# A decoder layer on one core: feed-forward weights quantised in pieces inside the cross-attention steps, the key rows of ones filled by GpSimd, and the query spread put first in SP's step

## The reference, cut to what matters

```python
x = x + attn(layernorm(x), gamma, Wq, Wkv, Wo)      # 16 heads, causal, rotary
x = x + xattn(layernorm(x), ctx, w_in, ..., 64)     # sequences of 512 places, 8 heads of 16,
                                                    # a band of 64 places on either side
x = x + ffn(layernorm(x), gate_w, down_w, ...)      # inner width 1408
def weight_quant(w):                                # ternary weights
    scale = 1.0 / clip(mean(abs(w)), 1e-5)
    return clip(round(w * scale), -1, 1) / scale
def bit_linear(x, w, g):
    return activation_quant(rms_norm(x, g)) @ weight_quant(w).T
# ffn: gate, up = split(bit_linear(x, gate_w, g1)); h = silu(gate) * up; bit_linear(h, down_w, g2)
```

## Time and profile before

| | |
|---|---|
| median of 3 runs | 1294.87 us (1294.2 to 1295.73) |
| the profiled execution, whole | 1297.97 us |
| its span | 1296.2 us |
| busy in the span | PE 83%, DVE 70%, ACT 43%, GpSimd 40% |
| self-attention ends | about 664 us |
| `setup_cross` | 664 to 684 us |
| `cross` | 684 to 1067 us |
| `setup_ffn` | 1067 to 1093 us |
| `ffn` | 1093 us to the end |

### The profile page before, as it was taken

How to read it: one execution, slowest core, us unless ns; L and a number is a source line. 1 busy time by engine, 2 the same in 40 slices (tenths; PEclk the granted TensorE clock), 3 DMA queues, 4 the chain that set the end, 5 groups by cost and what they waited for, 6 DMA issues and landing times. The chain is left out here.

```text
span 1296.2 us, 24877 instructions
## 1 busy us (share of the span) xinstructions
PE 1072.7 (83%) x9350; PEld 728.7 (56%) x9350; DVE 902.3 (70%) x1709; ACT 554.1 (43%) x887; POOL 515.8 (40%) x461
## 2 busy tenths in 40 slices
PE   0699999999999999999834899999999841777775
PEld 0677677677767667777511566666666520333332
DVE  5577777767777777778743656666666537788884
ACT  3133333333333333333311356656566645555554
POOL 3243434434343444434311134344343333566663
PEclk9989999999999999999975899999999965899998
DMA  8200000000000000000037456646566103000000
GB/s 306 108 1 1 1 1 1 1 1 0 0 0 0 1 0 0 0 0 1 1 135 200 99 117 125 144 120 139 132 130 147 27 24 112 9 24 24 24 25 25
DMA packets 35646, 71.52 MB, mean 55 GB/s; under 512 B 8544, under 2 KB 21344, under 8 KB 31456
## 3 DMA queue, kind: packets, MB, share of 16 engines
q1 hardware_dynamic: 32528, 61.82, 19.0%
q10 hardware_dynamic: 2208, 4.59, 1.0%
q0 software_dynamic: 816, 3.87, 0.8%
HBM read 53.09 MB, written 16.78 MB: 54 GB/s over the span
## 5 line engine op out<-in xcount | busy, mean ns | idle before, releaser
L382 PE MATMUL Yb<-Wo,a_oN 128*128 128x512 f32 x512 | 231.5, 595 | 0.0
L1019 DVE TENSOR_REDUCE mx<-Sm 128x4 f32<-128x768 f32 x128 | 122.4, 956 | 120.0 <-PE Sm L765 119.3
L468 POOL TENSOR_TENSOR a_ql<-a_rot,a_qh 128x512 fp32r<-128x512 f32 x64 | 83.6, 1312 | 183.3 <-ACT a_qh L437 183.3
L861 ACT ACTIVATE x_ex<-Se 128x768 f32<-128x768 f32 x128 | 102.8, 803 | 125.6 <-PE Se L765 125.5
L382 PEld LDWEIGHTS Yb<-Wo,a_oN 128*128 128x128 f32 x512 | 97.1, 191 | 98.5 <-issue 93.4
L315 PE MATMUL Qb<-a_xTh,WqH 128*128 128x256 f32 x512 | 147.0, 287 | 2.4 <-DVE a_vl L569 2.4
L316 PE MATMUL Qb<-a_xTl,WqH 128*128 128x256 f32 x512 | 145.9, 285 | 0.0
L317 PE MATMUL Qb<-a_xTh,WqL 128*128 128x256 f32 x512 | 145.9, 285 | 0.0
L429 ACT ACTIVATE Lb<-Lb 128x512 f32<-128x512 f32 x64 | 37.2, 582 | 253.9 <-PE Ob L374 253.9
L475 POOL TENSOR_TENSOR a_pl<-a_pr,a_ph 128x512 fp32r<-128x512 f32 x64 | 83.7, 1307 | 115.0 <-ACT a_ph L424 115.0
L315 PEld LDWEIGHTS Qb<-a_xTh,WqH 128*128 128x128 f32 x512 | 99.2, 194 | 6.4 <-DVE a_vl L569 3.8
(11 more groups left out here) (196 smaller groups left out, 2524.6 us busy)
## 6 DMA issues: line engine op xcount, KB each, us to landing
K<-k_parts SPq DMA_DIRECT2D x32, 256.0 KB, 7.9
q_parts<-x_qp SPq DMA_DIRECT2D x16, 384.0 KB, 2.6
k_parts<-x_kp SPq DMA_DIRECT2D x16, 384.0 KB, 2.6
Q<-q_parts SPq DMA_DIRECT2D x16, 384.0 KB, 5.0
gate_f<-in_gateT SPq DMA_DIRECT2D x1, 5632.0 KB, 16.1
X<-in_x SPq DMA_DIRECT2D x4, 1024.0 KB, 16.2
Wo<-in_Wo ACTq DMA_DIRECT2D x1, 4096.0 KB, 13.9
Q<-q_parts SPq DMA_DIRECT2D x16, 256.0 KB, 5.7
```

The costliest lines, as they stand in the source:

```text
L382: mm = pe.matmul(Yb[s % 2][:, :], oN[:, s % 2, i * P:(i + 1) * P], t["Wo"][:, HG * u + i, :], start=(i == 0), stop=(i == HG - 1))
L468: pool.tensor_tensor(rot_dst(False, True, par, r), rbuf(par, r)[:, 0:rot_width(r)], rot_dst(True, False, par, r).bitcast(F32), ALU.subtrac ...
L861: act.activation(ex[:, (PAIRS * b + p) % RING, 4 * hf * WIN:4 * (hf + 1) * WIN].rearrange("p (j c) -> p j c", j=2), Se[:, :, 0:2 * WIN], A ...
L1019: dve.tensor_reduce(mx[:, half, at:at + 4].rearrange("p (j a) -> p j a", j=2), Sm[:, :, 0:2 * WIN].rearrange("p j (a c) -> p j a c", a=2), ...
```

## The change

- The weights are cut in 12 pieces: the gate weights in 8 of 1408 columns a partition (704 KB each), the down weights in three of 1536 (768 KB) and one of 1024 (512 KB). Two staging buffers `w_stage` take turns. Every piece is read twice.
- In steps b = 0 to 5, ACT sums the absolute values of two pieces a step, behind the exponentials of slots 1 and 2. In steps 6 to 11, DVE scales and rounds two pieces (slots 0 and 1), ACT writes them as bf16 (slots 1 and 2), and DVE limits them (slots 2 and 7).
- In steps 4 and 6 the sum of a matrix is totalled over the partitions by a matmul in PE's slot 6, and DVE makes the factors from it in its slot 6.
- SP's step is in another order, and the loads of the pieces for the next step stand at its end.
- GpSimd writes the ones of `K` in step -1, after the keys' `low` of sequence 1, and PE waits for them before the first `Se`.
- `setup_ffn` keeps the layer norm's scales alone; SP issues the two norm weights there, not GpSimd.

```diff
+PIECES = [(0, i * F, (i + 1) * F) for i in range(2 * KD)] + [(1, a * D, min(a + 3, KF) * D) for a in range(0, KF, 3)]
+GATES = 2 * KD
+SUM_STEP, QUANT_STEP = 0, 6
...
-            sp.dma_start(t["gate_f32"][:, :].rearrange("p (k n) -> p k n", k=KD),
-                         dram["gateT"].rearrange("(k p) n -> p k n", p=P)).then_inc(t["gate_in"], 16)
...
-            for k in t["K"]:
-                dve.memset(k[ROWS:SHIFTED, :, :], 1.0)
...
+        def summed_at(b):
+            return [n for n in (2 * (b - SUM_STEP), 2 * (b - SUM_STEP) + 1) if 0 <= n < len(PIECES)]
+        def quantised_at(b):
+            return [n for n in (2 * (b - QUANT_STEP), 2 * (b - QUANT_STEP) + 1) if 0 <= n < len(PIECES)]
+        TOTALS = {SUM_STEP + GATES // 2: 0, SUM_STEP + len(PIECES) // 2: 1}
...
+                if (b, s) == (0, 0):
+                    wait(pe, k_ones, len(K))
...
+                    if s == 6 and b in TOTALS:
+                        i = TOTALS[b]
+                        wait(pe, v_ready, b + 2)
+                        wait(pe, w_sized, i + 1)
+                        pe.matmul(Ab[:, 0:1], t["ones"][:, :], w_size[:, i:i + 1], start=True, stop=True).then_inc(w_total, 1)
+                    if s == 7 and b in TOTALS:
+                        wait(pe, w_chain, 2 * TOTALS[b] + 1)
...
-                    if b == B - 1:
...
-                        act.activation(t["junk"][:, :], t["gate_f32"][:, s * n:(s + 1) * n], ACT.Abs,
-                                       accum_out=t["gate_part"][:, s:s + 1]).then_inc(t["gate_sized"], 1)
+                    for n in summed_at(b):
+                        if s == 1 + n % 2:
+                            i, lo, hi = PIECES[n]
+                            wait(act, w_in[n % 2], 16 * (n // 2 + 1))
+                            wait(act, w_summed, n)
+                            act.activation(w_stage[n % 2][:, 0:hi - lo], w_stage[n % 2][:, 0:hi - lo], ACT.Abs,
+                                           accum_out=w_part[:, n:n + 1]).then_inc(w_summed, 1)
+                    for n in quantised_at(b):
+                        if s == 1 + n % 2:
+                            i, lo, hi = PIECES[n]
+                            wait(act, w_rounded, n + 1)
+                            act.activation((t["gateQ"], t["downQ"])[i][:, lo:hi], w_stage[n % 2][:, 0:hi - lo], ACT.Copy,
+                                           bias=-MAGIC).then_inc(w_whole, 1)
...
+                if b == -1:
+                    wait(pool, k_low, b + 3)
+                    for i in range(len(K)):
+                        wait(pool, k_ones, i)
+                        pool.memset(K[i][ROWS:SHIFTED, :, :], 1.0).then_inc(k_ones, 1)
...
             def step(b):
-                if real(b + 2):
-                    keep("k", kp, b + 2, k_low, k_in, K_IN, k_kept)
-                if real(b):
-                    maxima_rows(b, 1)
                 if real(b - 2):
                     wait(sp, y_ready, b - 2)
                     sp.dma_start(ctxb[:, :], dram["ctx"][b - 2]).then_inc(ctx_in, 16)
                 if real(b + 2):
                     spread("q", Q, Q_RUNS, b + 2, q_kept, q_in)
+                    keep("k", kp, b + 2, k_low, k_in, K_IN, k_kept)
+                if real(b):
+                    maxima_rows(b, 1)
+                if real(b + 2):
                     spread("k", K, K_RUNS, b + 2, k_kept, k_in)
                 if real(b + 1):
                     maxima_rows(b + 1, 0)
                 if real(b + 3):
                     keep("q", qp, b + 3, q_low, q_in, Q_IN, q_kept)
+                for n in summed_at(b + 1):
+                    wait(sp, w_summed, n - 1)
+                    load(n)
+                for n in quantised_at(b + 1):
+                    wait(sp, w_summed, len(PIECES))
+                    wait(sp, w_whole, n - 1)
+                    load(n)
...
+            def factors(i):
...
+                wait(dve, w_total, i + 1)
+                dve.tensor_scalar(w_mean[:, i:i + 1], Ab[:, 0:1], 1.0 / (P * width), EPS, ALU.mult, ALU.max).then_inc(w_chain, 1)
...
+            def offset(n):
...
+                wait(dve, w_in[n % 2], 16 * ((len(PIECES) + n) // 2 + 1))
+                dve.tensor_scalar(piece, piece, w_inv[:, i:i + 1], MAGIC, ALU.mult, ALU.add).then_inc(w_rounded, 1)
+            def clip(n):
...
+                wait(dve, w_whole, n + 1)
+                dve.tensor_scalar(piece, piece, 1.0, -1.0, ALU.min, ALU.max)
...
+                    for n in quantised_at(b):
+                        if s == n % 2:
+                            offset(n)
+                        if s == 2 + 5 * (n % 2):
+                            clip(n)
```

More of the change, by code:

```diff
@@ L712, in cross @@
         oN = sb("oN", [P, D], F32)
+        w_stage = [sb(f"w_stage{i}", [P, WIDEST], F32) for i in range(2)]
+        w_part = sb("w_part", [P, len(PIECES)], F32)
+        w_size, w_mean, w_inv = sb("w_size", [P, 2], F32), sb("w_mean", [P, 2], F32), sb("w_inv", [P, 2], F32)
         gate = sb("gate", [P, D], F32)
@@ L1074, in step @@
                         rest(kp, kr, 1, b + 3, k_high, k_low, k_rest)
+                    if s == 3 and b in TOTALS:
+                        size(TOTALS[b])
+                    if s == 6 and b in TOTALS:
+                        factors(TOTALS[b])
+                    for n in quantised_at(b):
[3 more added lines that the diff above has]
+                            clip(n)
                     if b >= B - 1 and s % 2 == 1:
```

133 lines of the change are left out of this document (38 added, 95 removed).

## The result

| | before | after |
|---|---|---|
| median of the runs | 1295.30 us (4 runs) | **1307.85 us** (4 runs, 1303.47 to 1309.85) |
| the profiled execution, whole | 1297.97 us | 1303.47 us |
| its span | 1296.2 us | 1301.7 us |
| steps 0 to 11 | 243.8 us | 287.4 us |

A forecast was written before the change was run, and what follows sets the result against it. Cross steps were taken as PE-bound (92% busy, hiding waits, such as for the keys' spread), the setups by DVE fills and weight quantising. Terms -12.2 + 2.7 + 21 + 1.6 - 1.1 - 6 - 17.3 = -11.3 gave about 1283 us, range 1250 to 1306.

The forecast's parts named there:

- The setup before cross: Before the cross steps: without DVE's three fills the bias sum follows PE directly, -12.2 us.
- the fills on GpSimd: Three fills, 4.6 us each, stand in GpSimd's 21.5 us idle gap ahead of its first maxima work: 0.
- the pipeline's fill: Step -2: the queries' spread goes first, so the keys' keep is issued 2.6 us later; +2.7 us, bounds 0 and +6.
- the setup before the feed-forward steps: After cross: only aggregates, small instructions and two powers at 2.89 us remain; -17.3 us, or -14 with powers as long as before.
- step 15: Last cross step: eight ACT sums, 12.4 us, go, roughly half of them hidden; -6 us, between -4 and -11.
- replace each other, don't add: Steps 6 to 11: DVE's slot 0 load wait delays PE about 2 us, so it finds slot 4's rows nearly there.
- a time of some 1344 us: Rival "the small load is slow", chance 0.03: at the skill's price DVE and ACT wait for every piece, rows land T+19.
- a step lasts 19.05 + 2.0 + 1.0 = 22.05: Steps 0 to 11: no-DMA-wait base, slot 4 stall for maxima rows, clock loss; against 20.3, +21 us, bounds -15 and +44.
- its term for the factors: Steps 4 and 6: DVE stands in slot 6 for PE's total, then three small instructions; +1.6 us, bounds 0 and +4.
- compute alone: Steps 0 to 11: added ACT sums and DVE quantising cost nearly 0, up to +1 us a step if slots don't hold them.
- the sign turns: Steps 0 to 11: from 23.0 us a step on the change is slower, since the other terms give -32.3 us.
- The second rival: Steps 0 to 11, chance 0.25: the 2.9 us stall drops the clock every step; 24.2 us a step, +46, 1309 us.

The follow-up runs named there:

- the run with shifted work: The changed kernel with all sums, roundings, offsets and clips of the weights moved to later slots, mostly by two; median 1319.5 us.
- The run with the order alone: The kernel before with SP's step in the change's order (context rows and queries' spread ahead of keys' keep and maxima rows), no loads; 1295.5 us, ratio 0.9998.
- The run with the cut spread: The changed kernel with loads moved behind key spread and first-half maxima rows, and two of the queries' spread's three transfers put behind the second-half rows; 1253.2 us, the fastest.
- late loads: The changed kernel with the even piece loaded right behind the key spread and the odd one behind the first half's maxima rows; 1276.6 us.
- small work: The changed kernel with whole loads, but each sum, offset, rounding and clip on 32 columns instead of 1408 or 1536; 1319.8 us.
- the old order with the shift: The changed kernel with SP's step in its old order, loads last, and all work on the weights moved to later slots, mostly by two; 1277.9 us.

## Why the prediction was wrong

**Right, by its own steps.** The setup before cross (-12.5 for -12.2), the fills on GpSimd (0, hidden; 3.54 us each where 4.6 was estimated), the pipeline's fill (+2.7), the powers at 2.89 us and with them the setup before the feed-forward steps (-17.3), step 15 (-4.9 for -6), and no wait left on keys. The queue was drawn rightly up to the rows' issue, and "replace each other, don't add" was borne out by the run with shifted work. The rule of the Trainium skill in "DMA: Bandwidth & Descriptors", section Bandwidth, gave an estimate of 8.5 us for two pieces and a time of some 1344 us. The trace does not agree: the 704 KB loads land 6.0 us after their issue (median of 16, two at a time, behind a keep and with all latency), and the kernel took 1307.9.

**Wrong: the term "a step lasts 19.05 + 2.0 + 1.0 = 22.05".** It measured 23.95, and the runs take it apart. The run with the order alone has 20.2 us where the forecast had 19.05: the queries' spread ahead of the rows costs about what the keys' wait had cost, with no load near it. That is **+1.2 a step**, and the largest part; the mistake was to take a wait away from a step and call what is left a step without waits, when the new order has one of its own at slot 4. The loads add idle PE of (46.9 - 20.3) / 12 = 2.2 us for the 2.0 taken, **+0.2**. And PE's busy time rises by (240.5 - 222.3) / 12 = 1.5 us where 1.0 was taken for the clock, **+0.5**. The sum, 1.2 + 0.2 + 0.5, is the 1.9 us that were missing, 12 times, or 23 us, of which the forecast had 1.6 in its term for the factors. Between PE's own borders the step is 23.85, and the last part is 1.4 for 1.0. The run with the cut spread shows that the slower matrix work goes with the clock and not with the added instructions: over the same 4035 of them PE is busy for 224.1 us at 0.99.

That the loads' 2.2 us lies so near to 2.0 is in part luck, because it is not made up as forecast. In steps 6 to 11 PE waits 20.3 us for VectorE, 3.4 a step, where about 2 was expected. In steps 0 to 5 it waits 11.0 us for the rows, 1.8 a step, and 8.8 us for ScalarE, whose sums wait 15.6 us for their loads (10.8 for gate pieces, 4.8 for down pieces); the forecast named no such wait and put "compute alone" at nearly 0. With late loads ScalarE has the same sums and waits for no load, and PE waits 1.8 us for it in these steps. So the two waits that the forecast named are in their places; a third was left out, and the base and the price of the clock were set too low. At 23.95 us a step the sign turns, as the forecast's own balance says, which puts that point at 23.0.

The second rival, "slower: the stall costs the clock each time", came true in its number (24.2 us a step, 1309 us, against 23.95 and 1307.9), with 0.25 beside 0.46. What spoke for it was in the rows: the fall after a wait of only 1.11 us. Half of its own reason did not hold, since the wait of VectorE replaces the rows' wait instead of adding to it. The range of 1250 to 1306 ended just below the time: it left out half of that rival's cases.

**What stays open.** Why small work lengthened the steps; what it takes for a wait to cost clock; and why the fastest version still waits 10.0 us, in 9 places, for its rows. A kernel with the cut spread and no weights was not run, so what the loads still cost there is known only against the kernel before.

## What to carry to other kernels

A transfer added to a queue costs what stands behind it and is waited for next, and what its own reader waits, far more than its bytes: 1.4 MB a step cost 35 us over twelve steps in one place, and in another, with the query spread cut as well, the steps were no longer than with no load at all. Before moving transfers write down, for every one, when its data are ready and when its reader comes, and let the small, urgent one (here 12 KB of maxima rows) go ahead of anything large that is needed only a step later, cutting the large one if need be. And when a wait is subtracted to get a base, first ask the new order which wait stands next; the run with the order alone, which had no change in time, was what showed it.

## What the runs showed of the hardware

- A second queue did not protect a transfer. With the loads in ScalarE's queue and issued ahead of it, a keep of 384 KB in SP's took 6.5 us from issue to landing, against 5.2 behind the same loads in one queue, 3.2 ahead of them and 2.6 in the kernel before.
- Waits of PE can be paid twice. Its busy time for the same steps was 224.1 us at a mean clock of 0.99 and 240.5 at 0.92. But idle time alone does not say so: in the old order with the shift it was 33.4 us, and PE was busy for 226.6 us at 0.99:

```profile
706.93:966.92 259.99, 226.60 (x3998) 154.99 (x3998) 177.08 (x289) 174.21 (x258) 96.44 (x104) 0.99 0.75 189
```

- Filling 3 partitions with 4096 bf16 numbers took GpSimd 3.54 us and VectorE 3.47 us, nearly the same.
- Transfers issued by GpSimd cost it time, 36 us more busy time in twelve steps for six small transfers a step, and they landed no sooner (3.6 against 3.7 us).
